# The loop over batches of a transformer block, written out for every engine

## The reference

```python
xn = _layernorm(x)
# attention block, MLP and two layer norms
a = sliding_window_attn(xn, Wq, bq, Wk, bk, Wv, bv, Wo, bo)
h = layer_norm(a + xn, g1, b1)
f = gelu(h @ W1 + c1) @ W2 + c2          # 256 -> 1024 -> 256
attn_out = layer_norm(f + h, g2, b2)
# routed experts: one of 8 per row, each a 256 x 256 matrix
chosen = argmax(xn @ gate_w.T)
ffn_out = xn + (xn @ expert_w[chosen].T)
out = x + attn_out + ffn_out
```

## Time and profile before

| what | value |
|---|---|
| median of 3 runs | 1558.98 us (1557.52 to 1561.96) |
| span of the profiled execution | 1553.1 us, 34323 instructions |
| PE matmul busy | 1240.9 us, 80% of the span |
| VectorE (DVE) busy | 1071.5 us, 69% |
| ScalarE (ACT) busy | 739.8 us, 48% |
| GpSimd (POOL) busy | 739.9 us, 48% |
| mean granted TensorE clock | 0.913 |

### The profile page before, as it was taken

The page is one execution under the profiler, slowest core; times in us unless marked ns, Lnnn a source line. Parts: engine busy times, 40 slices in busy tenths (PEclk is TensorE's granted clock), DMA queues, the critical chain, the costliest instruction groups (busy, mean ns, idle before and its releaser), DMA issues.

```text
span 1553.1 us, 34323 instructions
## 1 busy us (share of the span) xinstructions
PE 1240.9 (80%) x10696; PEld 714.8 (46%) x10696; DVE 1071.5 (69%) x3743; ACT 739.8 (48%) x1356; POOL 739.9 (48%) x749
## 2 busy tenths in 40 slices
PE   0648885999678985999859997689858898599967
PEld 0424452735346353654527454373535535265435
DVE  8656775777757775867757677576766676587565
ACT  1305744366543744447443565426544374445642
POOL 6443745156531766037550474406752177504661
PEclk9959997999989997989979899798988899799979
DMA  7463056220733119130462206422082212912010
GB/s 237 92 139 118 3 117 122 76 92 29 144 79 100 57 69 166 50 112 13 108 131 69 99 8 145 91 83 83 33 156 75 88 57 74 162 48 94 2 28 28
DMA packets 89647, 135.00 MB, mean 87 GB/s; under 512 B 10209, under 2 KB 62305, under 8 KB 87393
## 3 DMA queue, kind: packets, MB, share of 16 engines
q1 hardware_dynamic: 83328, 115.91, 30.0%
q0 software_dynamic: 6144, 16.79, 4.4%
HBM read 74.47 MB, written 59.90 MB: 87 GB/s over the span
## 4 chain that ended last, share of the span: by engine, by line
PE 49%; DMA 17%; issue 11%; POOL 8%; DVE 8%; SPq 3%; ACT 3%; DVEq 0%; POOLq 0%; ACTq 0%
DMA pair_dram<-pool 9%; PE bank L1132 8%; PE bank L1035 8%; PE bank L1154 8%; PE bank L1036 7%; PE bank L1038 7%; PE bank L1181 6%; DMA q_s<-q_s 5%; DVE xn L604 2%; SPq L284 2%; DMA ys_dram<-xn 2%; PE bank L1102 2%; POOL x_sb L453 2%; POOL x_sb L451 2%; POOL rs L386 2%
## 5 line engine op out<-in xcount | busy, mean ns | idle before, releaser
L713 DVE CUSTOM_DVE_ANT_0 bank<-bank,mask 128x192 f32<-128x192 f32 x1024 | 337.3, 388 | 199.1 <-PE bank L1132 195.1
L943 ACT ACTIVATE pool<-bank 128x512 f32<-128x512 f32 x512 | 293.0, 597 | 118.9 <-PE bank L1154 113.2
L1132 PE MATMUL bank<-k_s,q_s 128*64 128x192 f16 x2048 | 175.3, 269 | 144.1 <-DMA q_s<-q_s 141.2
L440 POOL TENSOR_SCALAR_AFFINE_SELECT pool<-pool 128x512 f32<-128x512 f32 x256 | 172.2, 675 | 194.1 <-ACT pool L943 193.4
L1154 PE MATMUL bank<-q_s,k_s 128*128 128x256 f16 x1024 | 199.3, 290 | 28.7 <-issue 21.3
L389 POOL TENSOR_TENSOR rs<-ve,neghalf 128x1 f32<-128x1 f32 x64 | 36.9, 577 | 384.8 <-DVE ve L776 384.8
L1132 PEld LDWEIGHTS bank<-k_s,q_s 128*64 128x64 f16 x2048 | 77.8, 113 | 250.1 <-issue 226.9
L1181 PE MATMUL bank<-pool,v_a 128*32 128x256 f32 (+2 forms) x2560 | 161.1, 345 | 19.9 <-DVE pool L727 8.6
L989 ACT ACTIVATE pool<-bank,c1c 128x512 f32<-128x512 f32 x128 | 87.8, 686 | 169.5 <-PE bank L1038 132.5
L790 DVE TENSOR_TENSOR pool<-pool 128x512 f16<-128x512 f32 x128 | 106.7, 839 | 63.3 <-ACT pool L955 62.2
L713 DVE DVE_READ_ACCUMULATOR2_ANT m_sb<- 128x1 f32 x1024 | 144.6, 141 | 0.3
(11 more groups left out here) (149 smaller groups left out, 2511.1 us busy)
## 6 DMA issues: line engine op xcount, KB each, us to landing
pair_dram<-pool SPq DMA_DIRECT2D x32, 512.0 KB, 7.6
xn<-xs_dram SPq DMA_DIRECT2D x40, 384.0 KB, 3.7
ys_dram<-xn SPq DMA_DIRECT2D x120, 128.0 KB, 1.7
q_s<-pair_dram SPq DMA_DIRECT2D x48, 256.0 KB
k_s<-pair_dram SPq DMA_DIRECT2D x48, 256.0 KB
x_sb<-in_L_attn_x SPq DMA_DIRECT2D x8, 1024.0 KB, 5.7
res_dram<-x_sb SPq DMA_DIRECT2D x8, 1024.0 KB, 4.8
res_r<-res_dram SPq DMA_DIRECT2D x8, 1024.0 KB, 7.4
```

The source lines that it names most:

```text
L440: nc.gpsimd.affine_select(out=p, in_=p, compare_op=ALU.is_ge, fill=0.0, base=0, pattern=[[0, 4], [1, 2 * W]], channel_multiplier=-1).then_ ...
L713: ins = nc.vector.tensor_tensor_reduce(out=SB[u % 2][:, i * WIN:i * WIN + WIN], in0=SB[u % 2][:, i * WIN:i * WIN + WIN], in1=mask[:, v, :] ...
L943: nc.scalar.activation(prob[:, (k + 2) % 3, 2 * pu:2 * pu + 2, :], TB[u % 2][:, :].rearrange("p (h q) -> p h q", h=2), ACT.Exp, scale=EXP_ ...
L1132: mm = nc.tensor.matmul(SB[u % 2][W * bl:W * bl + W, i * WIN:i * WIN + WIN], q_s[:, h, W + w0:2 * W + w0], k_s[:, h // 2, w0:w0 + WIN], st ...
```

## The change

On all five engines the loop over batches 0 to 6 becomes a loop of the program that writes the code. Each engine's program holds its `turn` eight times over, one copy behind the other, with b a plain number in each. In `gelu_high` the test for a loop value becomes a test of the batch number, which is true in the same seven turns. The five hunks for the engines are alike; two are shown, with the condition.

```diff
@@ sync
             sorted_tiles(0)
-            with sp.Fori(0, NB - 1) as b:
+            for b in range(NB - 1):
                 turn(b, False)
             turn(NB - 1, True)
             sp.wait_ge(out_st.sem, out_st.at(NB - 1, 16))
...
@@ scalar
                 hf, c = divmod(u, FC)
-                if u == FC and not isinstance(b, int):
+                if u == FC and b < NB - 1:
                     act.wait_ge(pair_st.sem, pair_st.at(b + 1, 64))
...
@@ tensor
             pe.wait_ge(prep.sem, N_PREP)
-            with pe.Fori(0, NB - 1) as b:
+            for b in range(NB - 1):
                 turn(b, False)
             turn(NB - 1, True)
```

More of the change, by code:

```diff
@@ L521, in _ @@
             pool.wait_ge(prep.sem, N_PREP_D)
-            with pool.Fori(0, NB - 1) as b:
+            for b in range(NB - 1):
                 turn(b, False)
@@ L876, in _ @@
             dve.wait_ge(prep.sem, done)
-            with dve.Fori(0, NB - 1) as b:
+            for b in range(NB - 1):
                 turn(b, False)
@@ L1012, in _ @@
             act.wait_ge(prep.sem, N_PREP)
-            with act.Fori(0, NB - 1) as b:
+            for b in range(NB - 1):
                 turn(b, False)
```

## The result

| | before | changed |
|---|---|---|
| median, us | 1559.61 (1557.52 to 1561.96, 4 runs) | 1526.01 (1523.54 to 1526.44, 4 runs) |
| ratio, 95% interval | | 0.978 (0.9766 to 0.9794) |
| profiled span, us | 1553.1 | 1521.8 |
| instructions in the profile | 34323 | 30506 |
| mean granted clock | 0.913 | 0.929 |

The kernel is 2.2% faster; 1527.7 us was forecast. The profile's span was forecast at 1521.8 us and measured at 1521.8 us.

What follows compares the result with a forecast made beforehand. TensorE holds 49% of the chain, with "issue" pauses where its loop jumps back into turns 1 to 6. Pauses 16.61 us plus clock 14.72 us give 31.33 us: 1558.98 - 31.33 = 1527.7 us, range 1519 to 1543 us.

Steps and rivals of the forecast that it cites:

- The place and the size of the loss: Table load to first head copy, turns 1 to 6: 114.19 us should fall to 82.86, a gain of 31.33 us.
- Nothing is given back: From first head copy to next table load, the rest of each turn catches up none of the 5.22 us.
- Their own jumps are behind TensorE's: At turn starts, the jumps of SyncE, GpSimd, VectorE and ScalarE are hidden by TensorE's and cost nothing.
- The clock's share: In the stretches after the jumps, TensorE's lowered clock makes up 14.72 of the 31.33 us.
- the table load's own idle doesn't cost the clock: At turn starts without a jump, TensorE's 1.30 us idle during the table load leaves its clock up.
- rival 1: At turn starts the pause goes but the clock stays low: only 16.61 us gained, 1542.4 us; chance 0.13.
- Computed semaphore targets cost nothing: Inside the loop, waits whose targets are computed from the batch number cost 0 against constant targets.
- No cost for the longer code: Code of five engines about eight times as long fetches no more instructions; cost taken as 0.
- 2.3 MB on the instruction queues: Profile after: the instruction queues should move the same 2.3 MB as before.
- What lies around the span: Outside the profiled span: the median's 5.9 us above the 1553.1 us span isn't touched by the change.
- Same busy time on VectorE: Profile after: VectorE's busy time unchanged, as on ScalarE and GpSimd, with less on PE.
- Eight table loads: Profile after, at turn starts: eight loads of the exponential's table, each followed by its first exponential after 1.29 us.

Runs made afterwards that it cites:

- e10: The changed kernel as it is, run once more beside the kernel before: 1521.93 us, ratio 0.9788.
- e1: Kernel before with only TensorE's loop written out, the other four engines keeping theirs: 1547.88 us, ratio 0.9931.
- e3: Kernel before with all loops kept and hint_back_edge=True set on TensorE's loop: 1557.69 us, ratio 1.0006.
- e5: Kernel before with TensorE's and VectorE's loops written out, the other three kept: 1525.25 us, ratio 0.9805.
- e11: Kernel before with all loops but TensorE's written out, plus 12 matmuls nobody reads ending each looped TensorE turn: 1544.31 us, ratio 0.9921.
- e2: Kernel before with the loops of all engines but TensorE written out: 1554.86 us, ratio 0.9982.
- e6: Kernel before with all loops kept and the branch hint on TensorE's and VectorE's loops: 1542.97 us, ratio 0.9906.
- e8: Kernel before with all loops written out but VectorE's: 1542.57 us, ratio 0.9917.

## Why the prediction was right, step by step

- **The place and the size of the loss.** Right: 31.33 us were forecast for the six first stretches and 31.21 us came. That it fits to 0.1 us is luck, since the repeated kernel has 87.05 us there and not 82.98 (e10). Reading turn 0 and turn 7, which don't jump, against turns 1 to 6, which do, gave the price without any model of the jump.
- **Nothing is given back.** Right to 0.1 us over six turns. Inside the rests two parts changed against each other: from the last head copy to the gelu's table load turns 1 to 6 now take 38.0 to 39.0 us and took 36.0 to 37.7, and the part behind it is shorter by about as much. e1, e3 and e5 have 37.4 to 40.5 us there too, hint or not, so it doesn't take written-out code.
- **"Their own jumps are behind TensorE's", cost nothing.** Right for the whole change, where all five go, and wrong as a statement on what the pause is. I named ScalarE as the cover that could be gone, at 1.29 us. It was VectorE: its jump alone costs 17 us. The view where its own pause lies hidden is VectorE's timeline of the kernel before. There 3.15 us of idle time before its first maximum behind the jump to turn 1 are put down to TensorE's matmul:

```profile
319.82 0.37 DVE L713 CUSTOM_DVE_ANT_0 bank<-bank,mask 128x192 f32<-128x192 f32 x1 [3.15 <-PE bank L1132]
```

A releaser names the last to come, not all who would have been late.
- **The clock's share.** Right in that the pause's idle time is its cause. At turn 6 of the kernel before the granted clock is 0.50 from 1232 to 1241 us, after the 3.75 us without a matmul, and 1.00 again from 1242 us to the first head copy at 1248.62 us. In e11 keeping the array busy brought back 1.96 us a turn; the term had 14.72 / 6 = 2.45 us. The step "the table load's own idle doesn't cost the clock" held in 6 of 7 turns of the changed kernel and failed in turn 7 (15.02 us at 0.89), in e5 in turn 5, and in e10 in 3 turns. That is the +1.22 us above, and rival 1 in small: when such a turn comes is not known, and each costs 1.2 to 1.4 us.
- **Computed semaphore targets cost nothing.** The bound is e2, with four engines' targets constant: 1554.86 us, 0.2% below the kernel before, with an interval that reaches 1.0. e1 and e5 cover TensorE's and VectorE's together with their jumps. With all targets constant, the rests of turns 1 to 6 of the changed kernel, in which no jump lies, are the same in sum to 0.1 us.
- **No cost for the longer code.** Right in time. The expected 2.3 MB on the instruction queues was wrong: 1.44 + 0.51 = 1.95 MB, 15% less, with 11% fewer instructions in the profile. The loop fetched about everything it executed, and executed more.
- **What lies around the span.** The 5.9 us were a wrong reading. All runs taken since have a time of 1.7 to 1.9 us above their span, so the profiled execution of the kernel before took about 1554.9 us, below all four runs of the first set. The forecast of 1527.7 us mixes that span's parts with a slower median. The medians fell by 33.6 us and the profiled spans by 31.3; with single runs of the kernel before up to 20 us apart, that the forecast ended 1.7 us from the measured median is partly luck.
- **Same busy time on VectorE.** Wrong by 10 us: 1071.5 before, 1081.5 now. The gelu's low halves (line 790) went from a mean of 839 to 929 ns. In the other runs they take 854 to 962 ns, with loops and without. No stretch between the marks is longer for it; the cause was not tried. ScalarE, also forecast the same, has 7 us less (739.8 and 732.8 us).
- **Eight table loads.** Wrong: there are seven, turn 0 has none (see the end).

## What to carry to other kernels

A loop whose turn already stands written out once, ahead of it or behind it, holds its own control: lay the same stretch of both side by side, and the price of the jump can be read off, the clock that it costs TensorE included. TensorE and VectorE jump at the same time here and covered each other: TensorE's loop alone written out (e1) brought 0.7%, where the whole change brought 2.2%. So taking the jump from one engine, even the one that the chain names, may bring a third of the gain: take it from all that feed each other in the first microseconds of the turn. In this kernel these were the two engines with the longest code per turn. Two engines' loops written out were enough here, and kept the rest of the code short.

## What was not expected of the hardware

- A hint at the loop's head (e6) took TensorE's pause below 1.29 us and VectorE's to 0.74 us, and the whole kernel still came out 1.2% slower than with these two loops written out (1542.97 against 1525.25 us).
- Whether a jump pauses at all differs: ScalarE's showed nowhere with one turn a pass and paused for 3.09 us with two, where the pass is twice as long and the jump stands elsewhere in the code.
- Turn 0 has no table load when ScalarE's loop is written out. ScalarE's timeline of the changed kernel, where the load stood at 135.57 us before:

```profile
134.67 0.38 ACT L931 ACTIVATE xn<-bank 128x256 f32<-128x256 f32 x1 [0.45 <-PE bank L1038]
135.63 1.68 ACT L943 ACTIVATE pool<-bank 128x512 f32<-128x512 f32 x3 [0.58 <-PE bank L1154]
```

The same holds in e2, e8, e10 and e11, and in none of the runs whose ScalarE keeps its loop. The first exponential then comes 0.58 us after the last copy and not 1.31, which is 0.7 of the 1.25 us that the prologue gained.
